# A fused cross-attention and feed-forward layer on one core: new order of weight splits, operand splits and row tiles in the feed-forward stage

## What is computed

```python
# x [2, 2048, 512], context [2, 77, 512], 16 heads of 32
xq = layer_norm(x, qn_w, qn_b); ctx = layer_norm(context, cn_w, cn_b)
q = xq @ q_w; k, v = split(ctx @ kv_w)
attn = softmax(where(mask, -big, q k^T / sqrt(32)))
x = x + (attn v) @ proj_w + proj_b
h = layer_norm(x, n2_w, n2_b)
h = gelu(h @ fc1_w + fc1_b) @ fc2_w + fc2_b     # 512 -> 2048 -> 512
return x + h
```

## Time and profile before

| | us |
|---|---|
| median of 3 runs (lowest, highest) | 1178.64 (1175.17, 1181.35) |
| profiled execution, its own time | 1177.56 |
| its span | 1175.8 |
| busy: PE / PEld | 1096.9 / 919.2 |
| busy: DVE / ACT / POOL | 815.7 / 513.7 / 353.0 |
| chain that ended last, by engine | PE 70%, DVE 15%, issue 5%, ACT, DMA and POOL 3% each |

### The profile page before, as it was taken

One profiled execution on the slowest core, in us unless ns is written; L12 is line 12 of the kernel. 1 busy time (PEld: TensorE's weight loads), 2 busy tenths in 40 slices (PEclk: granted clock), 3 DMA queues, 4 the chain that ended last, 5 costly groups with the idle time before them and its releaser, 6 DMA issues.

```text
span 1175.8 us, 16878 instructions
## 1 busy us (share of the span) xinstructions
PE 1096.9 (93%) x5665; PEld 919.2 (78%) x5665; DVE 815.7 (69%) x1457; ACT 513.7 (44%) x1326; POOL 353.0 (30%) x255
## 2 busy tenths in 40 slices
PE   8999999999998778888889999998899999999998
PEld 6899998999897656666667777786777777878887
DVE  8888888888887646555668656757665667665655
ACT  5665565566655543333335233334333334312321
POOL 3345335534557445222153300033300033300000
PEclk9999999999998888888899999999999999999999
DMA  7111211211110155434344943432754333643411
GB/s 238 18 42 54 73 46 47 72 67 47 46 65 19 36 207 198 176 132 175 131 182 168 322 162 123 164 134 100 251 197 151 125 145 134 221 182 135 161 72 72
DMA packets 54755, 149.61 MB, mean 127 GB/s; under 512 B 13269, under 2 KB 21501, under 8 KB 46487
## 3 DMA queue, kind: packets, MB, share of 16 engines
q1 hardware_dynamic: 54095, 147.56, 35.4%
q10 hardware_dynamic: 584, 1.06, 0.3%
HBM read 108.13 MB, written 39.85 MB: 126 GB/s over the span
## 4 chain that ended last, share of the span: by engine, by line
PE 70%; DVE 15%; issue 5%; ACT 3%; DMA 3%; POOL 3%; SPq 1%; DVEq 0%; ACTq 0%; POOLq 0%
PE bank L1745 24%; PE bank L1715 22%; PE bank L1589 8%; PE bank L1547 6%; PE bank L1578 3%; PE bank L1528 3%; DMA out<-acc 2%; DVE acc L1387 2%; DVE xTl L1144 2%; DVE gT L1379 1%; PE bank L1724 1%; PE bank L1560 1%; DVE PTl L1161 1%; DVE w1r L1342 1%; DVE nmax L1138 1%
## 5 line engine op out<-in xcount | busy, mean ns | idle before, releaser
L1745 PE MATMUL bank<-w2r,gT 128*128 128x512 f32 x1536 | 385.8, 406 | 27.3 <-DVE acc L1387 27.3
L1745 PEld LDWEIGHTS bank<-w2r,gT 128*128 128x128 f32 x1536 | 293.6, 195 | 106.9 <-DVE acc L1387 46.3
L1715 PE MATMUL bank<-hop,w1r 128*128 128x512 f32 x1344 | 315.1, 393 | 13.0 <-DVE w1r L1342 7.2
L1715 PEld LDWEIGHTS bank<-hop,w1r 128*128 128x128 f32 x1344 | 254.7, 190 | 67.6 <-DVE w1r L1342 7.6
L1387 DVE TENSOR_TENSOR acc<-bank,acc 128x512 f32<-128x512 f32 x256 | 174.9, 689 | 113.2 <-PE bank L1745 111.1
L1374 DVE TENSOR_TENSOR ybuf<-bank,ybuf 128x512 f32<-128x512 f32 x224 | 145.2, 685 | 88.2 <-PE bank L1715 87.6
L1017 ACT ACTIVATE ybuf<-ybuf,cols 128x512 f32<-128x512 f32 x128 | 91.7, 716 | 169.4 <-DVE ybuf L1374 169.3
L1379 DVE TENSOR_TENSOR gT<-ybuf,gT 128x512 fp32r<-128x512 f32 x128 | 92.9, 745 | 52.6 <-ACT gT L1021 51.2
L851 ACT ACTIVATE S<-S,nmax 128x77 f32<-128x77 f32 x256 | 88.8, 354 | 49.1 <-DVE nmax L1138 49.1
L1010 ACT ACTIVATE ybuf<-bank 128x512 f32<-128x512 f32 x32 | 19.1, 598 | 189.0 <-PE bank L1715 189.0
L985 ACT ACTIVATE raw<-bank,cols 128x128 f32<-128x128 f32 x128 | 48.1, 455 | 101.4 <-PE bank L1724 101.4
(11 more groups left out here) (114 smaller groups left out, 1685.4 us busy)
## 6 DMA issues: line engine op xcount, KB each, us to landing
w1r<-w_scratch SPq DMA_DIRECT2D x24, 1792.0 KB, 7.4
w2r<-w_scratch SPq DMA_DIRECT2D x24, 1024.0 KB, 4.9
w_scratch<-w1r SPq DMA_DIRECT2D x8, 1792.0 KB, 6.9
xr<-in_x SPq DMA_DIRECT2D x16, 512.0 KB, 3.5
x_scratch<-xr SPq DMA_DIRECT2D x16, 512.0 KB, 2.8
hring<-x_scratch SPq DMA_DIRECT2D x32, 256.0 KB, 3.6
acc<-x_scratch SPq DMA_DIRECT2D x32, 256.0 KB, 4.3
w_scratch<-w2r SPq DMA_DIRECT2D x8, 1024.0 KB, 9.2
```

The lines of the kernel that those rows point to most:

```text
L1715: mm = pe.matmul(bank_[:, :], w1r[:, w1_slot(s), c, w, kk * P:(kk + 1) * P], hop[i][:, d, kk, :], start=(kk == 0 and n == 0), stop=(kk == ...
L1745: mm = pe.matmul(bY[t % 2][:, :], gT[s % 2][:, j, d, t * P:(t + 1) * P], w2r[:, s % 2, j, w, :], start=(n == 0), stop=(n == 5))
```

## The change

Computed values and the number of matmuls stay as they are. What moves:

- **Operand splits.** All seven `hop_lo` are on DVE; POOL's are gone. In set 7 they stand between the `y_add`s and `acc_add`s, and `hop_lo` 6 in set 0 of the next block, behind C11. `hop_hi` 0 to 3 stand before the second `gelu` on ACT. The `g_lo` of set 7 stand further back on DVE.
- **Second-layer weights.** `w2_hi` of set s goes on ACT from behind the four `w1_hi` to ahead of the first `gelu` of set s.
- **First-layer weights.** Set 1's are split at the end of attention (tail 2), and sets 2 to 7 in sets 1 to 6. On DVE the pairs of `w1_lo` stand one `acc_add` later, as do the norm steps of a set's second row tile.
- **Passage from attention.** On PE products 0 and 1 go from tail 1 to tail 2, and 2 and 3 back in tail 2. On DVE `hop_lo` and `w1_lo` go further back in both tails.
- **SP.** In a set of block 0: `store_w2`, `load_w2raw`, `load_h`, `store_w1`, `load_w1raw`; before, the stores and loads of both weights stood ahead of `load_h`. In blocks 1 and 2 `load_h` of tiles 0 and 1 stands ahead of all `store_out` and `load_acc`.

The diff, cut to its core:

```diff
@@ sync_program
         store_w1(0)
+        store_w1(1)
...
             for s in range(SETS):
+                if not last and s == 0:
+                    load_h(b + 1, 0)
+                    load_h(b + 1, 1)
...
                 if first:
+                    store_w2(s)
                     if s + 1 < SETS:
+                        load_w2raw(s + 1)
+                if not last:
+                    for t in TILES.get(s, ()):
+                        if t + 2 < BT:
+                            load_h(b + 1, t + 2)
+                if first:
+                    if 0 < s < SETS - 1:
                         store_w1(s + 1)
                     if s + 2 < SETS:
                         load_w1raw(s + 2)
-                    store_w2(s)
-                    if s + 1 < SETS:
-                        load_w2raw(s + 1)
@@ gpsimd_program, tail 2 and block
             if tail == 2:
-                hop_lo(0, 4)
-                hop_lo(0, 5)
                 w1_sums(1)
-                hop_lo(0, 6)
...
-                    if s == SETS - 1:
-                        for i in ON_POOL:
-                            hop_lo(b + 1, i)
@@ scalar_program, block
                     m1_copy(b, s)
+                if first:
+                    w2_hi(s)
+                if refill:
+                    hop_hi(b + 1, 0)
                 gelu(b, s, 0)
                 if refill:
-                    hop_hi(b + 1, 0)
+                    for i in range(1, 4):
+                        hop_hi(b + 1, i)
                 gelu(b, s, 1)
-                if refill:
-                    hop_hi(b + 1, 1)
                 gelu(b, s, 2)
                 gelu(b, s, 3)
                 if refill:
-                    for i in range(2, 7):
+                    for i in range(4, 7):
                         hop_hi(b + 1, i)
-                if first and s + 1 < SETS:
+                if first and 0 < s < SETS - 1:
                     for i in range(4):
                         w1_hi(s + 1, i)
-                if first:
-                    w2_hi(s)
@@ vector_program, block, set 7
+                if not last and s == SETS - 1:
+                    hop_lo(b + 1, 0)
+                    y_add(b, s, U2)
+                    hop_lo(b + 1, 1)
+                    y_add(b, s, U3)
+                    y_add(b, s, U4)
+                    y_add(b, s, C22)
+                    hop_lo(b + 1, 2)
+                    y_add(b, s, C12)
+                    y_add(b, s, C21)
+                    add(s, 0)
+                    add(s, 1)
+                    hop_lo(b + 1, 3)
...
+                    hop_lo(b + 1, 4)
+                    hop_lo(b + 1, 5)
+                    continue
+                if not first and s == 0:
+                    hop_lo(b, 6)
@@ tensor_program, tail
-            if tail == 2:
-                mul(0, 0, 2, first=True)
...
+            if tail == 2:
+                mul(0, 0, 0, first=True)
+                mul(0, 0, 1, first=True)
...
-            if tail == 1:
-                mul(0, 0, 0, first=True)
...
+            if tail == 2:
+                mul(0, 0, 2, first=True)
```

More of the change, by code:

```diff
@@ L569, in block @@
                     load_w1(b + 1, s + 2 - SETS)
[L570 to L576, removed]
                 if s == SETS - 1:
@@ L896, in step @@
                 hop_hi(0, 0)
-                w1_hi(0, 0)
+                hop_hi(0, 1)
             if tail == 2:
-                m1_copy(0, 0)
                 hop_hi(0, 3)
                 w1_hi(0, 3)
+                hop_hi(0, 4)
+                hop_hi(0, 5)
             if back:
@@ L912, in step @@
             if tail == 1:
-                hop_hi(0, 1)
+                w1_hi(0, 0)
                 w1_hi(0, 1)
             if tail == 2:
-                hop_hi(0, 4)
+                m1_copy(0, 0)
             if back:
@@ L945, in step @@
             if tail == 2:
+                for i in range(4):
+                    w1_hi(1, i)
                 hop_hi(0, 6)
@@ L1268, in step @@
                 h_stats(0, norm2)
-            if tail == 1:
-                hop_lo(0, 0)
-                w1_lo(0, 0)
-            if tail == 2:
-                y_add(0, 0, C11)
-                hop_lo(0, 3)
-                w1_lo(0, 3)
             if scores:
@@ L1287, in step @@
                 prob_lo(0, (1,))
+            if tail == 2:
+                hop_lo(0, 2)
+                w1_lo(0, 3)
             if scores:
@@ L1292, in step @@
                 prob_lo(1)
+            if tail == 2:
+                y_add(0, 0, C11)
             if scores:
@@ L1299, in step @@
                 masked(1, 3)
+            if tail == 1:
+                hop_lo(0, 0)
+                w1_lo(0, 0)
             if norm and prep is None:
@@ L1304, in step @@
                 prob_lo(2)
+            if tail == 2:
+                hop_lo(0, 3)
             if front:
@@ L1309, in step @@
                 prob_lo(3)
+            if tail == 2:
+                hop_lo(0, 4)
             if norm and prep is None:
@@ L1331, in step @@
                 recip(1)
+            if tail == 1:
+                hop_lo(0, 1)
+            if tail == 2:
+                hop_lo(0, 5)
+                w1_lo(1, 0)
+                w1_lo(1, 1)
             if back:
                 residual(0)
+            if tail == 2:
+                w1_lo(1, 2)
+                w1_lo(1, 3)
             if back:
                 residual(1)
+            if tail == 2:
+                hop_lo(0, 6)
         def w1_lo(s, i):
@@ L1400, in block @@
             for s in range(SETS):
-                refill = not last and s == SETS - 1
                 tiles = () if last else TILES.get(s, ())
@@ L1412, in block @@
                 add(s, 0)
-                if refill:
-                    hop_lo(b + 1, 0)
                 if len(tiles) > 0:
@@ L1425, in block @@
                     h_normed(b + 1, tiles[0])
-                if refill:
-                    hop_lo(b + 1, 1)
-                if first and s + 1 < SETS:
+                add(s, 2)
+                if first and 0 < s < SETS - 1:
                     w1_lo(s + 1, 0)
                     w1_lo(s + 1, 1)
-                add(s, 2)
+                add(s, 3)
                 if len(tiles) > 1:
@@ L1434, in block @@
                     v_hbn.wait(dve, b + 1, tiles[1])
-                add(s, 3)
+                add(s, 4)
                 if len(tiles) > 1:
                     h_variance(b + 1, tiles[1])
-                if refill:
-                    hop_lo(b + 1, 2)
-                if first and s + 1 < SETS:
+                if first and 0 < s < SETS - 1:
                     w1_lo(s + 1, 2)
                     w1_lo(s + 1, 3)
-                add(s, 4)
+                add(s, 5)
                 if len(tiles) > 1:
                     h_normed(b + 1, tiles[1])
-                add(s, 5)
-                if refill:
-                    hop_lo(b + 1, 3)
                 add(s, 6)
@@ L1670, in step @@
                 h_T(0, norm2)
-            if tail == 1:
-                mul(0, 0, 1, first=True)
             if tail == 2:
```

28 lines of the change are left out of this document (12 added, 16 removed).

## The result

| | before | after |
|---|---|---|
| median of 4 runs each (lowest, highest), us | 1178.76 (1175.17, 1181.35) | 1139.37 (1137.46, 1141.51) |
| profiled execution, its span | 1177.56, 1175.8 | 1137.7, 1135.9 |

The ratio is 0.9668, 95% interval 0.9634 to 0.9702. The forecast was 1142, its own range 1132 to 1152: 36.8 under the kernel before were forecast and 39.4 measured.

A forecast was written before the change was run, and what follows sets the result against it. TensorE is 70% of the chain, so time is won only where it waits or runs at its lower clock. Terms -0.5 - 5.6 - 19.6 - 7.8 + 0.5 - 3.5 = -36.5 on 1177.56 give 1141.1; median 1142, range 1132 to 1152.

The forecast's parts named there:

- A: Passage from attention to block 0's set 1: attention ends at 415, set 1 starts at 435.2, net -0.5 us.
- the gain of the tail is eaten by the wait for `w2raw`: At the passage: the 8 us taken off attention's end go to waiting for the load of `w2raw`.
- bound by its weight traffic: Rival, chance 0.05: weight traffic, not order, limits block 0; sets 2 to 6 keep 142 less a few; 1165 us.
- the table switch: At the passage, on ACT: the rows say 1.31 us with the load; the skill's 2.66 would end 1.4 higher.
- B: Set 1 of block 0: from 32.6 to 27.0 us, -5.6 (bounds -8 and 0).
- C: Sets 2 to 6 of block 0: earlier `w2_hi` removes stall and slow clock; 142.2 to 122.6 us, -19.6.
- The surcharge of set 6: Set 6 of block 0: POOL makes T1 to T4 beside `w1_lo`, adding 6.4 us to 20.6.
- D: Set 7 of blocks 0 to 2: POOL's low parts go, all on DVE; -7.8 us, and +0.5 in following sets 0.
- E: Set 1 of blocks 1 and 2: `load_h` first, against waits for `hring`; -3.5 us for both (bounds -7.5 and 0).
- the half that POOL's bias sums were to keep: Set 1, blocks 1 and 2: POOL adds bias to eight `acc` tiles before the inverse root, so half was taken.
- POOL and DVE block each other: Rival, chance 0.17: DVE subtractions wait out POOL's; attention ends no earlier, sets 2, 4, 6 lose 2 each; 1156 us.

## Why the prediction held, step by step

- **A. Right in number, wrong in what it means.** Attention ends at 414.9 and set 1 starts at 435.2, both within 0.2. (The forecast's sum is 20.0 behind the end of attention, and it goes on with 20.2; by its own sum the term is -0.7.) The wait for `w2raw` holds the start of set 1, as forecast. The step "the gain of the tail is eaten by the wait for `w2raw`" fell: without that wait the kernel is no faster, since the DMA engines are full until about 440 and set 2 starts at 461 anyhow. The gain is eaten by 9.7 MB of traffic, 3.7 of it the stores of `w1r`. I had read loads singly, by their time to landing, and never the DMA share of the stretch. The rival "bound by its weight traffic" said this of sets 2 to 6, where it is not so, and not of the passage, where it is.
- On the table switch the rows were right: 1.28 for the load, 1.31 from the copy's end (427.68) to the GELU (428.99). The 2.66 that the Trainium skill, page "ScalarE: Activation LUTs", section "What ACT_TABLE_LOAD costs", gives with a drain did not show here.
- **B.** -5.6 forecast, -6.6 measured. It ends where the traffic of A ends, so it is not a term of its own: start of set 1 and length of set 1 trade against each other.
- **C. Right in mechanism and size.** 23.8, 24.0, 23.8, 24.0 and 27.0 forecast; 23.4, 23.6, 23.0, 23.6 and 28.4 measured. The stall that it names is what went: moving `w2_hi` back brings it back, link by link. Missing was that the gain hangs on SP's order: alone, the move makes the kernel 1.1% slower. The surcharge of set 6 was 7.8 in place of 6.4, and came in the main from three `g_lo`, 5.3 us late, and only 1.6 from `w1_lo`.
- **D.** -7.8 + 0.5 forecast, -8.1 measured. The sets 7 gave -9.5 (21.5, 20.6, 20.6), and the sets after them took back 1.4: -0.9, and +2.3 for DVE's jump back of the loop, which the old slack had hidden. Right in direction, and close by luck in part: 1.4 of the -9.5 is TensorE's stop at the jump in block 1, which this execution of the changed kernel happens not to have and others near it do.
- **E.** -3.5 forecast, -4.1 in the profile, all of it in block 2. The wait for `hring` that the forecast named is gone, and comes back when the load goes back. The size is luck in part: the half that POOL's bias sums were to keep was right for this execution, and others with the early load keep 2.4 to 3.7 us more.
- The rival "POOL and DVE block each other" is true in set 6 of block 0 and not in the tail, where attention ended 8.3 earlier.

## What to carry to other kernels

When several engines' waits meet at one place, look at the DMA share of that stretch first. If it is full, as here, removing a wait may only move it, and what paid here is the order of the queue, with stores that nobody waits for behind the loads. Moving a consumer forward needs its load moved forward in the same edit; in sets 2 to 6 here the pair gained 16 us and the move alone lost 6. Once a kernel is tight, look at the ends of hardware loops, where an engine that used to arrive early may now arrive last. And look at more than one execution before you credit a term with 2 us.

## What the runs showed of the hardware

- A hardware loop's jump leaves DVE idle for 3.2 us (782.55 to 785.73) where the same work written out has none. It shows in the chain as "issue" and "DVEq" at the line of the loop. TensorE stood 1.4 to 2.4 us at the same place in eight profiled executions and not at all in four others that have the loop, nor in the two without it.
- Two DVE subtractions of 128x512, both inputs in SBUF, took 5.02 us beside POOL's subtractions and 1.28 without.
- With all 16 DMA engines busy (share 0.98 to 1.04) this core moved 388 to 444 GB/s between 425 and 440 us, and 343 to 356 between 422 and 426; the time to landing of a 256 KB load of `w2raw` went from 5.2 to 15.3 us with what was queued ahead of it.
